# A graph layer's edge loop: one of forty row fetches a round done by TensorE instead of GpSimd's gather, in rounds 4 to 38 of layer 0

## What is computed

```python
edge_index = jnp.stack([src, dst])
# layer 0, attention: every node is also its own neighbour (a loop is appended to src and dst)
h = x @ W
e = leaky_relu((h @ att_src)[src] + (h @ att_dst)[dst], 0.2)
m = segment_max(e, dst); e = exp(e - m[dst])
alpha = e / (segment_sum(e, dst)[dst] + 1e-16)
x = layernorm(x + tanh(segment_sum(h[src] * alpha[:, None], dst) + bias))
# layer 1, messages
h = gelu(x @ W_pre + b_pre)
z = x + segment_sum(h[src] * edge_attr, dst)
x = layernorm(x + z + gelu(gelu(z @ W1 + b1) @ W2 + b2))
```

## Time and profile before

| | us |
|---|---|
| median of 3 runs | 3726.49 (3724.31 to 3727.02) |
| profiled execution | 3724.54 |
| its span, first to last instruction | 3722.8 |
| POOL busy / DVE / PE / ACT in the span | 2781.1 / 2438.3 / 2393.6 / 1283.2 |
| mean granted PE clock | 0.709 of full speed |

### The profile page before, as it was taken

How to read it: one execution, slowest core, us unless ns; L and a number is a source line. 1 busy time by engine, 2 the same in 40 slices (tenths; PEclk the granted TensorE clock), 3 DMA queues, 4 the chain that set the end, 5 groups by cost and what they waited for, 6 DMA issues and landing times.

```text
span 3722.8 us, 66966 instructions
## 1 busy us (share of the span) xinstructions
PE 2393.6 (64%) x16704; PEld 1951.7 (52%) x16705; DVE 2438.3 (65%) x6240; ACT 1283.2 (34%) x3893; POOL 2781.1 (75%) x2950
## 2 busy tenths in 40 slices
PE   6433343434344444444445988989888989999888
PEld 3333333333333333333334777777776777777776
DVE  7444444444466666566666777777777788888886
ACT  5433343434445555555553111111111221111222
POOL 7777777777777777777775777777777777777776
PEclk7555555555555555555557999999999999999998
DMA  5222221222222222222223343443334343444332
GB/s 102 43 42 42 41 44 42 44 42 43 42 43 44 43 44 43 43 44 45 44 45 99 93 94 90 95 94 94 95 91 96 93 96 91 97 95 99 93 95 70
DMA packets 351632, 254.26 MB, mean 68 GB/s; under 512 B 254125, under 2 KB 279218, under 8 KB 351387
## 3 DMA queue, kind: packets, MB, share of 16 engines
q0 software_dynamic: 94016, 146.16, 17.8%
q1 hardware_dynamic: 242753, 99.71, 11.7%
q10 hardware_dynamic: 14618, 6.14, 0.6%
HBM read 244.43 MB, written 7.25 MB: 68 GB/s over the span
## 4 chain that ended last, share of the span: by engine, by line
POOL 60%; issue 24%; ACT 4%; DVE 4%; PE 3%; DMA 2%; ACTq 1%; DVEq 1%; POOLq 0%; SPq 0%
POOL rows L690 60%; ACT onehot L747 1%; DMA rows<-table,src_i 1%; DMA src_i<-in_src_dram 1%; PE bank L1086 1%; ACT L790 1%; ACTq L740 0%; ACT pair L767 0%; DVE score L1361 0%; PE bank L1029 0%; PE bank L962 0%; ACT rowu L796 0%; DVE bst L1399 0%; ACT unused L790 0%; DVE newp L1352 0%
## 5 line engine op out<-in xcount | busy, mean ns | idle before, releaser
L690 POOL DMA_INDIRECT rows<-table,src_i x2850 | 2694.8, 946 | 896.0 <-issue 859.5
L1086 PE MATMUL bank<-node,hot 128*128 128x288 bf16 x9310 | 1228.4, 294 | 28.1 <-issue 16.5
L995 PE MATMUL bank<-onehot,rows 128*97 128x72 f32 (+1 forms) x3048 | 584.9, 369 | 814.9 <-ACT onehot L777 814.9
L1086 PEld LDWEIGHTS bank<-node,hot 128*128 128x128 bf16 x9310 | 932.2, 101 | 282.4 <-issue 20.9
L995 PEld LDWEIGHTS bank<-onehot,rows 128*97 128x97 f32 x3048 | 530.8, 281 | 854.4 <-issue 792.5
L1505 DVE TENSOR_SCALAR hot<-node,key 128x642 bf16<-128x642 int16 x1862 | 870.3, 539 | 130.8 <-PE bank L1086 80.0
L900 ACT ACTIVATE pair<-dst_i 128x8 f32<-128x8 int32 x196 | 35.2, 180 | 1175.3 <-DVE rows L1531 904.3
L747 ACT ACTIVATE onehot<-iota,far_dst 128x72 f32 (+1 forms) x1564 | 384.4, 328 | 23.0
L1339 DVE SCALAR_TENSOR_TENSOR other<-onehot,bank 128x576 f32<-128x576 f32 (+1 forms) x196 | 121.9, 622 | 404.1 <-ACT bank L760 335.4
L1073 PE MATMUL bank<-onehot,rows 128*96 128x40 f32 (+1 forms) x3128 | 306.8, 256 | 88.4 <-DVE rows L1536 50.6
L1073 PEld LDWEIGHTS bank<-onehot,rows 128*96 128x96 f32 x3128 | 295.8, 170 | 110.1 <-issue 88.7
(11 more groups left out here) (204 smaller groups left out, 1931.1 us busy)
## 6 DMA issues: line engine op xcount, KB each, us to landing
attr<-in_edge_attr_dram SPq DMA_DIRECT2D x190, 336.0 KB
rows<-table,src_i POOLq DMA_INDIRECT x2850
node<-in_src_dram SPq DMA_DIRECT2D x195, 64.0 KB
attr<-in_edge_attr_dram SPq DMA_DIRECT2D x190, 48.0 KB
dst_i<-in_dst_dram SPq DMA_DIRECT2D x200, 4.0 KB
src_i<-in_src_dram SPq DMA_DIRECT2D x195, 4.0 KB
src_i<-in_src_dram SPq DMA_DIRECT2D x190, 3.5 KB
dst_i<-in_dst_dram SPq DMA_DIRECT2D x190, 3.5 KB
```

The lines of the kernel that those rows point to most:

```text
L690: pool.indirect_dma_start(rows[:, u, j * width:(j + 1) * width], None, table, bass.IndirectOffsetOnAxis(ap=src_i[:, u, j:j + 1], axis=0))\
L995: last = pe.matmul(total[:, 0:w], rows0(u, it)[:, j, 0:D1], wide(weights, w)[:, j, :], start=j == 0, stop=j == most - 1)
L1086: last = pe.matmul(p_got[t], hot[:, c % HOTS, i, t * P:(t + 1) * P], tab[:, a, :, :].rearrange("p k d -> p (k d)"), start=a == 0, stop=a = ...
```

## The change

In layer 0, from round 4 (`FROM0`) to 38, tile 7 of slot 0 is no longer gathered by POOL. PE fetches it by 49 matrix products with a bf16 table in three parts, as layer 1 does. One tile in 40 is moved (`BOOKED0` is 1), 35 tiles in all.

- **The table.** Rows of `x1` (26 node blocks into `attr`, 2 into the free end of `x1`, 21 into `hot`) are split into three bf16 parts in nine steps, at the groups of `SPLIT_AT` in rounds 1 and 2: per step up to two ACT copies and two DVE subtractions.
- **Comparisons.** For every round from 4 on, DVE makes 49 comparisons of 128 columns (`marks0`, ten pieces of 4 or 5). Two pieces are done in every group, the first between L1344 and L1318, the second at the group's end.
- **Products.** PE does the two pieces' products (`fetch0`, 128 x 294) behind the second half of its window sum.
- **Taking.** At a round's last group DVE waits for all ten pieces and adds the three parts into `rows` of slot 0 (`taken0`); ACT's copy of source scores of slot 0 waits for it. ACT shortens the tile's node numbers to int16 (`shorten_src0`), SP loads them, 64 KB to all partitions (`load_src0`), and loads the indices of slot 0 in three DMAs where there were two.
- **Around it.** PSUM: the fetched tile takes bank 1, what lay there moves to bank 0, and `p_node2` shares bank 6 with `p_node`. Rounds 0 to 3, 18, 37 and 38 are written out. No chunk is due before round 4.

```diff
+BOOKED0 = 1
+FROM0 = 4
+ERA0 = 10
...
+        TABLE0 = [(b, e, flat[0], 0) for b, e in shares(0, ROOM[0], 4)] + \
+            [(ROOM[0], ROOM[0] + ROOM[1], flat[1], ROOM[0])] + \
+            [(b, e, flat[2], sum(ROOM)) for b, e in shares(sum(ROOM), HOT_B, 3)]
+        PIECE0 = [NB * c // ERA0 for c in range(ERA0 + 1)]
...
-        p_top, p_topb, p_newp = bank[0][0:WIN, 0:P], bank[1][:, 0:WIN], bank[1][:, P:P + WIN]
+        p_top, p_topb, p_newp = bank[0][0:WIN, 0:P], bank[0][:, P:P + WIN], bank[0][:, P + WIN:P + 2 * WIN]
...
@@ gather, on POOL
-                    for j in range(TILES - (e is e1 and booked(it, u))):
+                    for j in range(TILES - (booked(it, u) if e is e1 else booked0(it, u, ws[0]))):
...
@@ on ACT
+            def shorten_src0(it):
+
+                act.wait_ge(q_src, 16 * BOOKED0 * (it + 3 - FROM0))
+                if not first_era(it, SLOTS - 1):
+                    act.wait_ge(q_hot, (it + 2 - FROM0) * ERA0)
+                act.activation(src16_0, src_all0, ACT.Copy).then_inc(q_src16, 1)
...
@@ on PE
+            def fetch0(it, u, c, n):
+
+                pe.wait_ge(q_hot, piece_no(it, u, c) + 1)
...
+                for i, a in enumerate(range(PIECE0[c], PIECE0[c + 1])):
+                    for t in range(n):
+                        last = pe.matmul(p_got0[t], hot0[:, c % HOTS, i, t * P:(t + 1) * P], table0_block(a),
+                                         start=a == 0, stop=a == NB - 1)
+                last.then_inc(q_done, 1)
...
                 window_sum(p_acc0, onehot[:, u, :], it, u, range(TILES // 2, TILES), w).then_inc(e0.acc, 1)
+                if in_era(era_at(it, u)):
+                    for c in pieces_at(u):
+                        fetch0(it, u, c, fetched_at(it, u, w))
...
@@ on DVE
+            def taken0(it, n):
+
+                v.wait_ge(q_done, (it + 2 - FROM0) * ERA0)
+                for k in range(n):
+                    last = v.tensor_reduce(rows0(k, it + 1)[:, TILES - 1, :], p_got0[k].rearrange("p (k d) -> p d k", k=3),
+                                           AX.X, ALU.add)
+                last.then_inc(q_out, 1)
+
+            def marks0(it, u, c, n):
+
+                if c == 0:
+                    v.wait_ge(q_src16, it + 3)
+                if not first_era(it, u) or c >= HOTS:
+                    v.wait_ge(q_done, piece_no(it, u, c) - HOTS + 1)
+                for i, a in enumerate(range(PIECE0[c], PIECE0[c + 1])):
+                    last = v.tensor_scalar(hot0[:, c % HOTS, i, 0:n], src16_0[:, 0:n], key[:, a:a + 1], None,
+                                           ALU.is_equal)
+                last.then_inc(q_hot, 1)
...
+                if ahead:
+                    marks0(back, at_u, pieces_at(at_u)[0], fetched_at(back, at_u, w) * P)
                 top_node(st, t0, g + 1, w)
...
                 if g is not LAST:
+                    if split_step(it, u) is not None:
+                        split_rest0(split_step(it, u))
+                    if ahead:
+                        marks0(back, at_u, pieces_at(at_u)[1], fetched_at(back, at_u, w) * P)
+                    if u == SLOTS - 1 and in_era(it + 1):
+                        taken0(it, booked_in(it + 1, w))
```

More of the change, by code:

```diff
@@ L282, in __init__ @@
                 self.dst = sems(f"e{n}_dst", SLOTS)
-                self.attr = sems(f"e{n}_attr", SLOTS)
+                self.attr = sems(f"e{n}_attr", SLOTS) if n else None
                 self.rows = sems(f"e{n}_rows", SLOTS)
@@ L287, in __init__ @@
                 self.acc = sem(f"e{n}_acc")
-                self.v = sem(f"e{n}_v")
+                self.v = None if n else sem(f"e{n}_v")
         class Top:
@@ L304, in __init__ @@
                 self.w = sem(f"{n}_w")
+        q_src = sem("q_src")
+        q_src16 = sem("q_src16")
+        q_hot = sem("q_hot")
+        q_done = sem("q_done")
+        q_out = sem("q_out")
         h_zero = sem("h_zero")
@@ L389, in x_here, with groups @@
                 eng.wait_ge(s_x[-1], 16)
-        def groups(eng, body, after_round=None, alone=0):
+        def groups(eng, body, after_round=None, alone=0, apart=0):
             def one(it, w, then):
@@ L402, in groups @@
             one(SLIM_ROUNDS - 1, SLIM, WIN)
-            with eng.Fori(SLIM_ROUNDS, ROUNDS - 1) as it:
+            with eng.Fori(SLIM_ROUNDS, ROUNDS - 1 - apart) as it:
                 one(it, WIN, WIN)
-            one(ROUNDS - 1, WIN, WIN)
+            for it in range(ROUNDS - 1 - apart, ROUNDS):
+                one(it, WIN, WIN)
             return body(LAST, ROUNDS, 0, (WIN,))
         def named(it, u, ws):
-            return f"{u}_{ws[0]}_{isinstance(it, int)}_{it is ROUNDS}_{first(it)}_{second(it)}"
+            return f"{u}_{ws[0]}_{it if isinstance(it, int) else 'loop'}"
         due_regs = {}
@@ L417, in due @@
         def due(eng, k, body, packed=None):
+            if isinstance(k, int) and k < HELD:
+                return
             if packed is None:
@@ L558, in body @@
                         return
+                    if not attrs and booked0(it, u, ws[0]):
+                        load_split(g, u, e)
+                        return
                     if g is LAST:
@@ L637, in _ @@
             store_table()
-            groups(sp, load_edges(e0, False), alone=2)
+            groups(sp, load_edges(e0, False), alone=FROM0, apart=1)
             sp.wait_ge(e0.free, GROUPS + SLOTS)
@@ L693, in gather @@
                 return body
-            groups(pool, gather(e0, table0, D2), alone=2)
+            groups(pool, gather(e0, table0, D2), alone=FROM0, apart=1)
             pool.wait_ge(m_st, STORED)
@@ L851, in _ @@
             act.sem_inc(m_st, 16)
+            act.sem_inc(m_g, 1)
+            act.sem_inc(q_src16, FROM0)
             act.sem_inc(f_st, 16)
@@ L861, in middle_due @@
                 table_for(ACT.Exp, 3)
-            groups(act, weights, middle_due, alone=2)
+            groups(act, weights, middle_due, alone=FROM0, apart=1)
             rest(act, middle, middle_last)
@@ L1037, in _ @@
             spread_top(t0, 1, SLIM)
-            groups(pe, attend, alone=2)
+            groups(pe, attend, alone=FROM0, apart=1)
             def unread(n):
@@ L1347, in attend @@
                     score_column(u + 1)
+                back, at_u = (it, u - 1) if u > 0 else (-1 if first(it) else it - 1, SLOTS - 1)
+                ahead = g is not LAST and in_era(era_at(back, at_u))
+                if ahead:
+                    marks0(back, at_u, pieces_at(at_u)[0], fetched_at(back, at_u, w) * P)
                 top_node(st, t0, g + 1, w)
@@ L1478, in _ @@
             v.wait_ge(s_w, 16 * 8)
+            v.tensor_copy(key[:, :], key_i[:, :])
             set_window(0, load_window(0), 0)
-            prev = groups(v, attend, middle_due, alone=2)
+            prev = groups(v, attend, middle_due, alone=FROM0, apart=1)
             left = due_chunks(v, ROUNDS)
```

158 lines of the change are left out of this document (135 added, 23 removed).

## The result

The changed kernel takes 3747.04 us (median of 5 runs, 3746.02 to 3748.42), the kernel before in the same series 3724.67 (3724.26 to 3727.02). The ratio is 1.0058, 95% interval 1.0048 to 1.0069: slower by 22.4 us, where the forecast was faster by 15. The time lies in the range that was given (3684 to 3750), and on the other side of the time before. The profiled execution is the one of 3747.04, with a span of 3745.2.

What follows compares the result with a forecast made beforehand. POOL's gathers were taken to bound layer 0, consumers only rounds 30 to 38: -18.7 (rounds 4 to 18) - 13.7 (19 to 29) + 17 (30 to 38) = -15.4, so 3711 us; forecast's own range 3694 to 3718, 8-of-10 range 3684 to 3750.

Steps and rivals of the forecast that it cites:

- POOL, 35 x 1.25: One gather of 40 removed in rounds 4 to 38, 1.25 us each: 43.7 us of POOL's time.
- Splitting the table: Nine splitting steps in rounds 1 and 2 add 1.5 us to groups with 3.7 to spare, so they cost nothing.
- Rival C: Gain and loss cancel, comparison 0.187 to 0.202 us or gathers slowed by DVE's SBUF reading: within 0.2%, chance 0.14.
- The comparison, 0.17 us: Each DVE comparison of 128 int16 columns takes 0.17 us, between bounds of 0.12 and 0.28; ten in most groups.
- Rival B: DVE bounds the whole window of 72 if a comparison costs 0.21 us: +15 us, time 3735 to 3780, chance 0.20.
- The period, 8.13: Consumers' time for a group whose rows are already there grows by 0.68, from 7.45 to 8.13 us.
- PE hidden by 0.2 us: PE's second piece, sum and transpose take 3.3 us against DVE's own 3.5 to L1318, so products stay covered.
- `taken0`, 1.85 a round: At each round's end DVE waits 1.3 us for the tenth piece, then sums three parts in 0.45: 1.85 with semaphore.
- 55 x 8.13 ... + 5 x 12: Rounds 19 to 29: consumers need 527 us, POOL 536, so POOL decides and 13.7 us are won.
- 45 x 8.13 ... + 84: Rounds 30 to 38, seven chunks: consumers need 467 us against POOL's 439, so consumers decide and 17 us are lost.
- Waits of POOL: POOL waits for DMAs of src_i 10 to 30 us in all, only from 1500 us on.
- Rival A: POOL decides to the end, by comparisons of 0.13 us or less or faster PE: 3683 to 3693, chance 0.21.

Runs made afterwards that it cites:

- slim_only: The changed kernel with the fetched tile in rounds 4 to 18 alone, rounds 19 to 38 gathering all forty tiles: 3709.72 us, ratio 0.9958 to the kernel before.
- one_product2: The changed kernel with one PE product after each piece of comparisons instead of five: 3727.90 us, ratio 1.0005 to the kernel before.
- before_unrolled2: The kernel before, all 40 gathers a round, with rounds 19 to 38 written out instead of a loop: 3726.83 us, ratio 1.0003.
- window72_unrolled: The changed kernel with rounds 19 to 38 written out instead of a loop, look-up kept: 3719.19 us, ratio 0.9983 to the kernel before.

## Why the prediction was wrong, step by step

- **POOL, 35 x 1.25.** Right: 2815 gathers, 948 ns. Rounds 4 to 18: from 4.5 us behind to 13.6 ahead is 18.1, forecast 18.7.
- **Splitting the table, "nothing".** Wrong by 4.5 us, lost by the end of round 3. What was lost was POOL's own time: its gathers were longer there, from 50 to 300 us,

```profile
L821 POOL DMA_INDIRECT rows<-table,src_i x152 | 145.8, 959 | 46.3 <-issue 46.0 <-DMA src_i<-in_src_dram 0.3
L816 POOL DMA_INDIRECT hot<-table,src_next x40 | 39.6, 989 | 12.2 <-issue 11.9 <-DMA src_i<-in_src_dram 0.3
```

  against 945 and 952 ns before: 152 x 14 + 40 x 37 ns = 3.6 us. slim_only, which splits the table too, has 958 and 984. That the splitting slows them wasn't tested by itself. Rival C had named gathers slowed by DVE, but for the comparisons, beside which they take 948 to 949.
- **The comparison, 0.17 us.** Right: five take 0.90 us, of which the last 0.25 or so is its own tail, one after another 0.163. The estimate that the prediction worked out from the Trainium skill's rate (VectorE: DVE Perf Modes, "The perf-mode tier table"), 0.155, was nearer still. Rival B had the right place, DVE in the whole window of 72, and a sum of +15, but its price of 0.21 was not met: B's outcome came without B's cause. In the same way it is luck that 3747.04 lies inside the stated 3684 to 3750; the upper end stood for a dearer comparison.
- **The period, 8.13.** Right, slightly high: median 8.0, in 80 groups 645.8 us where the consumers alone took 600.3, so 45.5 for a forecast of 54.
- **PE hidden by 0.2 us.** Right, by one_product2: with a fifth of the products the group inside a round stays at 8.0.
- **`taken0`, 1.85 a round.** Its own size was right (1.50 + 0.46). But the forecast's 1.85 + 0.68 at a round's end is 2.53, and measured against the consumers alone it is 3.0 with a chunk and 4.5 without, 12 x 3.0 + 7 x 4.5 = 68 us where 19 x 2.53 = 48 were forecast. With a chunk nothing of it is hidden, though "DVE waits for PE anyway"; without one the pause behind it also grew, from 3.83 to 4.91: the look-up, which had lain under DVE's last two operations, now stands bare behind `taken0`, and the time behind the branch is 3.35 to 3.63 us in place of 2.7 to 3.1. Why that is longer isn't shown.
- **The failed step: "Consumers need ... 55 x 8.13 ... + 5 x 12" and "45 x 8.13 ... + 84", with no term for a round's end without a chunk.** What failed is the consumers' need: it left out what a round's end costs by itself. The consumers alone, unchanged, need 913 for the 99 intervals and not 882: 7 x 2.9 = 20 us are those ends (the loop's return above all, then the wait for ACT with its table reload), 12 x 0.56 = 7 the ends with a chunk, and 80 x 0.05 = 4 the groups inside. I took 7.45 from groups behind a chunk and the chunk from the earlier trace rows, and never looked at a round's end without one, whose cost the waits for rows in the other groups made up for. The earlier trace rows have "issue 25.2" in 44 groups, ahead of that very line, and I counted only the 19.3. Of the 25.2, 3.73 and 3.57 are the two ends without a chunk in that stretch, and the rest are six ends behind a chunk.
- **The sum.** Forecast for the 99 intervals after: 882 + 54 + 48 = 984; measured 1026.4, 31 more in the base, 20 more at the ends, 9 less inside. POOL's own need, by slim_only's 988.5 less 20 x 1.25, is some 964. So the consumers decide from round 19, not 30: 1026.4 - 990.1 = +36 where +3 was forecast (-13.7 + 17), with the -14.3 at which round 19 begins that makes the +22 of round 38.
- **Waits of POOL, "10 to 30 us in all, only from 1500 us on".** Wrong for the same reason: they are 60.2 us, and 7.4 of them lie between 1000 and 1250 us already, where the line had 0.6:

```profile
L821 POOL DMA_INDIRECT rows<-table,src_i x196 | 186.1, 949 | 64.6 <-issue 57.3 <-DMA src_i<-in_src_dram 7.4
```

- **The clock.** The main forecast was right: in the changed kernel it is 0.50 with PE busy 66% of 1250 to 1500 us. The rule by which the prediction let it rise at least in part under this load does not come out here. Rival A's time of 3683 to 3693 was reached only by leaving the comparisons out.

## What to carry to other kernels

A consumer's need is read where it is the bound; at every place where it waits for the producer something may lie under the wait, at loop ends above all. Before moving work to it, take the producer away (here seven gathers of eight) and time the consumer alone: one run gave the 31 us that the account had missed. A wait that is taken away can come back behind another engine: the loop's return gave 28 us of 49, since ACT's row stood behind it. Moved work has a density at which both sides are busy: with a tile moved in all rounds the kernel lost 22 us, with the same and a lighter round's end (rounds written out, the reload only behind a chunk) it won 18, and with three rounds of four in the window of 72 it won 28.

## What the runs showed of the hardware that I had not expected

- **A loop's return is dear on DVE and cheap on ACT, POOL and SP.** Behind the branch of the rounds' loop DVE's next instruction came after 2.7 to 3.6 us (3.38 at 1784.25), in every round, with a chunk or without; ACT's came after 0.2 at the same loop's return, POOL's and SP's after 0.1. DVE stood still 3.83 us at a round's end in the loop and 0.80 in code written out. The Trainium skill (Runtime: NRT & Kernel Launch, "Instruction fetch mechanics") says that a taken branch to a far target forces a fetch before the engine goes on, and that kernels prefer unrolling. DVE's pause agrees; that it is such a fetch, and why the others don't have it, no run here shows. before_unrolled2 adds that it is worth nothing (ratio 1.0003) where another engine decides.
- **A table reload that changes nothing still costs.** `ACT_TABLE_LOAD` took 1.28 us at each round's end, without a chunk too, where no other table had been used since; putting the call behind a chunk alone took it away there, and with it one of four reloads at an end with a chunk, and gave 11.7 us. The Trainium skill (ScalarE: Activation LUTs, "What ACT_TABLE_LOAD costs") adds 1.38 us for a drain at a switch to a different set; here the next activation starts 1.30 us after the load does (1581.14 to 1582.44), and as long after a load behind a chunk, where other functions had run since (1413.03 to 1414.33 in window72_unrolled). No run shows the drain.
- **PE's busy share doesn't tell its clock.** From 1250 to 1500 us the granted clock was 0.58 without comparisons, with PE busy 155 us of 250, and 0.50 with them, with PE busy 165; with the faster clock the same products also take less of the time. 0.58 is a mean (stretches of 50 us between 1000 and 1400 us have 0.50 to 0.67), so the clock was at the higher level for a part of the time. What lifted it isn't shown.
- **Series can differ by half in time.** In the series of 5488 us POOL's gathers kept their 949 ns, but their indices came late: 1937 us of waiting; in that of 5527 us they took 945 ns, with 1737 us of waiting. Whether it was the chip or something beside the kernel isn't shown.
